# Routed experts' rows added into the second layer's rows by the gathering transfers, and the loads of two lanes released by the last expert's product, in a two-layer decoder kernel

## The chip, the cores and the metric

The kernel runs on one core of one Trainium2 chip. The metric is the device time of one execution in microseconds; several executions are timed, and one more is run under the profiler. The engines are TensorE (PE), VectorE (DVE), ScalarE (ACT), GpSimd (POOL) and SyncE (SP, which only issues transfers here). Each takes its instructions in the order in which they are written; semaphores hold them until what they need is there. A transfer that GpSimd issues can fetch its rows by a table of row numbers (a gather).

## What is computed

Two decoder layers on x of 8 x 256 rows of 256 values. Layer 1 ends with a feed-forward part of routed experts; layer 2 takes its sum, normalised, through attention by Fourier transforms, cross attention and a feed-forward part with three-valued weights.

```python
def _L0_ffn_ref(...):
    x = hidden_states.reshape(-1, Dm)
    logits = x @ router_w
    expert_idx = jnp.argmax(logits, axis=-1)
    score = jax.nn.sigmoid(jnp.max(logits, axis=-1))
    xs = x * score[:, None]
    for e in range(n_experts):
        m = (expert_idx == e)[:, None]
        xe = jnp.where(m, xs, 0.0)
        h = jax.nn.silu(xe @ gate_w[e]) * (xe @ up_w[e])
        out = out + jnp.where(m, h @ down_w[e], 0.0)
    shared = jax.nn.silu(x @ shared_gate_w) * (x @ shared_up_w) @ shared_down_w
    return (out + shared)

x = _layernorm(x + _L0_attn_ref(x, ...), axis=-1)
x = _layernorm(x + _L0_xattn_ref(x, ctx_512, ...), axis=-1)
x = _layernorm(x + _L0_ffn_ref(x, ...), axis=-1)
x = _layernorm(x + _L1_attn_ref(x, ...), axis=-1)
x = _layernorm(x + _L1_xattn_ref(x, ctx_512, ...), axis=-1)
x = _layernorm(x + _L1_ffn_ref(x, ...), axis=-1)
```

The change touches the third of these lines: the sum of x, the shared part and the routed part, and its layer norm.

## The kernel before

**Units and lanes.** The rows are cut into 8 units of 256 rows (one batch entry each), held as 128 partitions x 2 rows of 256 values. Layer 1 works on units 0 to 7. Layer 2 works on the same rows as units 8 to 15. A lane is the set of on-chip tiles that one unit uses; layer 2 has four lanes, for units 8 to 11; units 12 to 15 reuse them. The lanes of units 8 and 9 lie in the area that the profile calls `wide`, those of 10 and 11 in `first`.

**Experts.** Layer 1 leaves, per unit, x plus the shared part in the DRAM tensor `x_mid` (the mid stores), and sends each row to a slot of `sent_rows` by its expert. 23 tiles of 128 such rows then go through `x_t` (transpose), `x_gu`, `x_h`, `x_b` (transpose), `x_dn` (product back), `x_out` (ScalarE's copy) and `x_st` (SyncE's store to the DRAM tensor `made_rows`). Tile 22 is the last. `made_at` says for each row of a unit where in `made_rows` its result lies.

**Into layer 2.** For unit u, in before:

- `ld` (SyncE) loads the unit's rows of `x_mid` into B.y, once all made rows and all mid stores have landed (`opened`), and for units 12 to 15 once the lane's former unit has had its last normalised rows made (`ln_x` of u-4, part 3);
- `gt` (GpSimd, L2314 on) gathers the unit's rows of `made_rows` by two indirect transfers into a tile of its own, B.got, once the same stores have landed, and for units 12 to 15 once the lane's former `res` part 0 has read B.got;
- `res` part 0 (VectorE, L1969) adds: B.y = B.y + B.got, once both have landed;
- `ln` (VectorE, L1927 to L1933) takes the statistics, `ln_pow` (GpSimd, L2275 and L2277) the power -1/2, `ln_x` (ScalarE, L1647) the normalised rows;
- `turn` part 0 (TensorE, L1077 with c_identity) transposes them, `ft` (L1070 with w_dft_hi) takes the Fourier transform, `nr` and `nk` normalise it (GpSimd's L2371 and L2376), `cs` (L1476) sums along the rows, `cs_v` (GpSimd L2383 to L2385), `vt` and `proj` part 1 go back; then come `q` (L1070 with w_lq_hi), `sc`, `ex`, `pv` and `proj` part 2 of cross attention, and `gu` (L1494), `hf` and `proj` part 3 (L1252) of the feed-forward part.

**Weights made meanwhile.** The weights of layer 2 are made on the chip from the inputs, in eight parts by heads and columns. `ha` (L1144), `hk`, `hw`, `hb`, `hc` fold the cross attention's matrices for a pair of heads (heads 6 and 7 are the last). `f_16`, `f_sc` and `f_gt` (VectorE L1910 to L1919), `f_q` (GpSimd L2332 to L2339, four instructions for a part), `fw` and `fw_c` make the three-valued weights. `ld_f` and `ld_h` are their loads; a wide area of the chip's memory is shared, so that `ld_f` or `ld_h` waits for an earlier `fw_c`.

**The order.** Every step above is one part in `lay_plan()`, with an engine, a length and the parts that it follows. `p.settle(n_banks, passes, seed)` lays the parts out and so draws the order of the instructions on every engine at once; the seed shakes their urgency. The emitters then write each engine's instructions in that order. `keep_warm` puts dummy matmuls (`bank<-c_all_ones`, L1461) where the layout shows TensorE idle. A change of one number in the table can thus move instructions everywhere.

## Time and profile before

| | before |
|---|---|
| median of three runs | 640.63 us (639.15 to 644.22) |
| the profiled execution, own time | 638.61 us |
| its span in the profile | 637.3 us |
| mean granted clock of TensorE | 0.979 |
| TensorE matmul busy | 574.4 us (90%) |
| VectorE busy | 480.8 us (75%) |
| ScalarE busy | 386.7 us (61%) |
| GpSimd busy | 374.3 us (59%) |

The span is the stretch that the profile shows; the execution's own time has 1.3 us around it. Busy shares are means over stages that are bound by different things: layer 1 to 210 us, mostly the experts' tiles from 210 to 284, the first tokens of layer 2 from 284 to 335, and from there layer 2 with all lanes filled. The timelines name an instruction by its start, its length, its line, the tile that it writes and those that it reads; a bracket gives how long its engine sat idle before it and what ended that.

### The profile page before, as it was taken

The numbers are of one execution on the slowest core, as the hardware profiler recorded it, in microseconds if no ns is written. First come the engines' busy times: TensorE is split into PE (matmuls) and PEld (weight loads), VectorE is DVE, ScalarE is ACT, GpSimd is POOL, SyncE is SP. The second block draws the span as 40 slices with busy tenths as digits, with TensorE's granted clock in tenths as the row PEclk, the third lists the DMA queues.
The fourth block names the chain that finished last, engine by engine and source line by source line (L and its number), as shares of the span: only waits on it lengthen the run. The fifth ranks groups of instructions, "written<-read, shape, count | busy, mean of one in ns | idle before, by whom it ended". The sixth has DMA issues, their size and how long they took to land. (4 is left out here: it accounts for less than half of the span.)

```text
span 637.3 us, 14620 instructions
## 1 busy us (share of the span) xinstructions
PE 574.4 (90%) x5400; PEld 445.5 (70%) x5400; DVE 480.8 (75%) x1286; ACT 386.7 (61%) x826; POOL 374.3 (59%) x468
## 2 busy tenths in 40 slices
PE   5789989988889799876989999999999999999995
PEld 4656767767666465553546888886788768889894
DVE  4673767776688798866779877697988997876656
ACT  3668667667766455541765565665747655655763
POOL 3436445556783267578998654572675634333896
PEclk9999999999899899998989999999999999999999
DMA  9753221102455244426211000001000000000001
GB/s 257 231 147 80 60 84 60 42 19 68 141 145 163 76 124 150 126 92 182 79 38 35 1 2 2 7 29 35 1 9 27 14 21 2 1 2 2 2 1 67
DMA packets 50418, 41.75 MB, mean 66 GB/s; under 512 B 15642, under 2 KB 48924, under 8 KB 50332
## 3 DMA queue, kind: packets, MB, share of 16 engines
q1 hardware_dynamic: 46444, 35.08, 18.6%
q0 software_dynamic: 1536, 4.20, 2.1%
q10 hardware_dynamic: 2368, 1.54, 0.9%
q8 instruction: 44, 0.72, 0.5%
q14 instruction: 26, 0.21, 0.1%
HBM read 31.49 MB, written 10.35 MB: 66 GB/s over the span
## 5 line engine op out<-in xcount | busy, mean ns | idle before, releaser
L1821 DVE TENSOR_TENSOR first<-bank,first 128x512 f16<-128x512 f32 (+3 forms) x141 | 76.1, 556 | 22.5 <-ACT first L1656 5.9
L2297 POOL TENSOR_TENSOR first<-first 128x512 f16<-128x512 f32 x44 | 51.9, 1181 | 42.4 <-ACT first L1708 32.6
L1077 PE MATMUL bank<-c_identity,first 128*128 128x128 f32 (+1 forms) x353 | 58.9, 284 | 9.2 <-DMA first<-in_x 3.1
L1070 PE MATMUL bank<-wide,first 128*128 (+4 forms) x199 | 54.2, 282 | 11.9 <-DVE first L1821 5.1
L1077 PEld LDWEIGHTS bank<-c_identity,first 128*128 128x128 f32 (+1 forms) x353 | 40.3, 141 | 20.3 <-DMA first<-in_x 3.7
L1071 PE MATMUL bank<-wide,first 128*128 (+4 forms) x199 | 53.8, 280 | 0.0
L1072 PE MATMUL bank<-wide,first 128*128 (+4 forms) x199 | 52.9, 279 | 0.0
L2275 POOL TENSOR_TENSOR first<-first,minus_half 128x2 f32<-128x2 f32 x30 | 21.6, 719 | 46.5 <-DVE first L1933 46.5
L1077 PE MATMUL bank<-c_identity,wide 128*128 128x128 f32 (+3 forms) x203 | 34.1, 291 | 9.2 <-DMA c_all_ones<-const_all_ones 7.1
L1821 DVE TENSOR_TENSOR wide<-bank,wide 128x512 f16<-128x512 f32 (+3 forms) x57 | 35.0, 635 | 9.0 <-ACT wide L1687 3.5
L1070 PEld LDWEIGHTS bank<-wide,first 128*128 128x128 f16 (+1 forms) x199 | 19.2, 98 | 24.6 <-issue 16.5
L1647 ACT ACTIVATE wide<-wide 128x256 f32<-128x256 f32 x32 | 17.4, 593 | 31.0 <-POOL wide L2277 30.9
L1077 PEld LDWEIGHTS bank<-c_identity,wide 128*128 128x128 f32 (+3 forms) x203 | 23.9, 146 | 16.2 <-DMA c_all_ones<-const_all_ones 7.1
L1700 ACT ACTIVATE first<-bank 128x512 f16<-128x512 f32 x44 | 26.2, 596 | 11.1 <-PE bank L1328 5.4
L1998 DVE TENSOR_REDUCE first<-bank 128x8 f32<-128x512 f32 x44 | 27.6, 681 | 6.1 <-PE bank L1290 3.7
L2332 POOL TENSOR_TENSOR wide<-wide 128x768 bf16<-128x768 bf16 x8 | 13.1, 1642 | 31.5 <-DVE wide L1919 31.5
L1494 PE MATMUL bank<-first,w_fgu 128*128 128x256 f16 x256 | 29.8, 273 | 0.6 <-DVE first L2219 0.6
L1494 PE MATMUL bank<-wide,w_fgu 128*128 128x256 f16 x256 | 30.1, 273 | 0.0
L2396 POOL TENSOR_TENSOR wide<-wide 128x512 f16<-128x512 f32 x16 | 18.6, 1161 | 19.0 <-ACT wide L1797 19.0
L1708 ACT ACTIVATE first<-bank 128x512 f32<-128x512 f32 x44 | 26.3, 597 | 5.7 <-POOL first L2297 5.5
L2297 POOL TENSOR_TENSOR wide<-wide 128x512 f16<-128x512 f32 x16 | 18.5, 1158 | 17.9 <-ACT wide L1708 15.4
L1070 PE MATMUL bank<-first,wide 128*128 128x256 f16 (+1 forms) x98 | 25.9, 271 | 2.4 <-DVE first L1821 2.4
(471 smaller groups left out, 2106.3 us busy)
## 6 DMA issues: line engine op xcount, KB each, us to landing
first<-sent_rows SPq DMA_DIRECT2D x20, 128.0 KB, 2.0
made_rows<-first SPq DMA_DIRECT2D x20, 128.0 KB, 1.8
wide<-in_L_ffn_gate_w SPq DMA_DIRECT2D x8, 256.0 KB
wide<-in_L_ffn_up_w SPq DMA_DIRECT2D x8, 256.0 KB
wide<-in_L_ffn_down_w SPq DMA_DIRECT2D x8, 256.0 KB
wide<-in_L_xattn_Wq SPq DMA_DIRECT2D x8, 256.0 KB
wide<-in_L_xattn_Wo SPq DMA_DIRECT2D x16, 128.0 KB
wide<-in_L_ffn_w_gate_up SPq DMA_DIRECT2D x8, 256.0 KB
```

Source lines behind the costliest of these rows:

```text
L1070: mm(o, lhs[0], rhs[0], start=start, stop=False)
L1071: mm(o, lhs[0], rhs[1], start=False, stop=False)
L1072: return mm(o, lhs[1], rhs[0], start=False, stop=stop)
L1077: last = nc.tensor.transpose(view[0:m, c0:c0 + n], src, kc["identity" if dt == F32 else "identity_bf"][0:n, 0:n])
L1494: last = mm(b[:, n * S:(n + 1) * S], k.w_fgu[:, c, at:at + P], B.xT[part][:, c, :], start=(c == 0 and part == 0), stop=(c == C - 1 and par ...
L1700: fn(lane(u).ph[g % 2], scores(u, g)[:, :], ACT.Exp, scale=0.25 if u < NB else 1.0).then_inc(says("ex_h"), 1)
L1708: fn(lane(u).pf, scores(u, g)[:, :], ACT.Exp, scale=0.25 if u < NB else 1.0).then_inc(says("ex_f"), 1)
L1821: return V.tensor_tensor(lo, whole, hi, ALU.subtract)
L1998: V.tensor_reduce(o, b, AX.X, ALU.max).then_inc(says("max_v"), 1)
L2275: pool.step(G.tensor_tensor(B.rstd, B.rstd, k.minus_half, ALU.pow))
L2297: G.tensor_tensor(B.pl[r], B.pf, B.ph[r], ALU.subtract).then_inc(says("ex_l"), 1)
L2396: G.tensor_tensor(lo, B.hf, hi, ALU.subtract).then_inc(says("hf_lo"), 1)
```

## The change

B.got is gone. The gather of a unit waits for the unit's own load and then adds the rows of `made_rows` into B.y on the way (`compute_op=ALU.add`). The eight adds of `res` part 0 are gone, and `ln` part 0 waits for the gather. The loads of units 8 and 9 no longer wait for the made rows, but for the last expert's product `x_dn` 22 and the mid stores; those of 10 to 15 wait as before. A few lengths in the planner's table are changed (`f_sc` 170 to 185, `f_gt` 195 to 186, `rt_xs` 140 to 114, `tb_tok` 498 to 560, left out of the diff below), and the order is drawn with 38 passes and seed 81.

```diff
--- before.py
+++ after.py
@@ -499,9 +499,10 @@
             return (name, o, g) if o is not None else None
 
         gate = [("x_in_st", n, 0) for n in range(NT)] + [("in_mid", v, 0) for v in every]
-        p.add("gt", u, 0, "POOL", 200, gate + [("tb_tok", 0, 0), old("res", 0)], k)
-        p.add("in_gt", u, 0, "AIR", 200, [("gt", u, 0)])
-        p.add("ld", u, 0, "SP", 45, gate + [("in_mid", i, 0), old("ln_x", 3)], k)
+        p.add("gt", u, 0, "POOL", 200, gate + [("tb_tok", 0, 0), ("in", u, 0)], k)
+        p.add("in_gt", u, 0, "AIR", 220, [("gt", u, 0)])
+        over = [("x_dn", NT - 1, 0)] + [("in_mid", v, 0) for v in every] if i < 2 else gate
+        p.add("ld", u, 0, "SP", 45, over + [old("ln_x", 3)], k)
         p.add("in", u, 0, "AIR", 250, [("ld", u, 0)])
         p.add("ld_ctx", u, 0, "SP", 90, gate + [old("rope")], k)
         p.add("in_ctx", u, 0, "AIR", 250, [("ld_ctx", u, 0)])
@@ -510,8 +511,7 @@
         p.add("kd_lo", u, 0, "POOL", 43, [("kd_hi", u, 0)], k)
         chain("kt", u, 0, [("rope", u, 0), old("sc", 3)], k, pe=20, hi=29, lo=28)
 
-        p.add("res", u, 0, "DVE", 70, [("in_gt", u, 0), ("in", u, 0)], k)
-        norm(u, 0, k)
+        norm(u, 0, k, "in_gt")
         chain("turn", u, 0, [("ln_x", u, 0)], k)
         for t in range(T):
             p.add("ft", u, t, "PE", 136, [("turn_lo", u, 0), ("pd_lo", 0, 0), ("pd_lo", 0, 1)], k, 1, ("ft_raw", u, t) if t else ("nr", u, 0))
@@ -568,7 +568,7 @@
         p.add("res", u, 3, "DVE", 122, [("rm_pow", u, 0), ("proj", u, 3)], k)
         norm(u, 3, k)
         p.add("st", u, 0, "SP", 45, [("ln_x", u, 3)], k)
-    p.settle(8, 37, 38)
+    p.settle(8, 38, 81)
     p.keep_warm(80, 0.7, 900)
     return p
 
@@ -808,7 +808,7 @@
             return v if dt == F32 else v.bitcast(dt)
 
         tn = "p (t n) -> p t n"
-        B.x, B.y, B.got = (tile([T, D]) for m in range(3))
+        B.x, B.y = (tile([T, D]) for m in range(2))
         B.xT = (tile([C, S], F16), tile([C, S], F16))
         B.ctx, B.kv, B.rot = (tile([DC]) for m in range(3))
         B.kv2 = tile([P])
@@ -988,7 +988,12 @@
                 sp.wait_ge(*done("rt_xs", u - FIRST))
             load(B.x, unit_rows(A["x"], u), dma["x"][u % FIRST])
         else:
-            opened(u)
+            if u < NB + 2:
+                sp.wait_ge(*done("x_dn", NT - 1))
+                for n in range(FIRST):
+                    sp.wait_ge(dma["mid"][n], 16 * turns_of(n))
+            else:
+                opened(u)
             if u >= NB + LANES:
                 sp.wait_ge(*done("ln_x", u - LANES, 3))
             load(B.y, unit_rows(k.x_mid, u - NB), dma["x"][u % LANES])
@@ -1920,7 +1925,10 @@
 
     def ln(u, n):
         B = lane(u)
-        dve.wait_ge(*done("proj" if u < NB and n < 2 else "res", u, n))
+        if u >= NB and n == 0:
+            dve.wait_ge(dma["got"][u % LANES], 32 * visit(u))
+        else:
+            dve.wait_ge(*done("proj" if u < NB and n < 2 else "res", u, n))
         dve.wait_ge(*done("pm_pow", 0))
         y = summed_rows(k, u, n)
         for t in range(T):
@@ -1963,10 +1971,6 @@
         if u < NB:
             dve.wait_ge(*done("proj", u, n))
             last = V.scalar_tensor_tensor(B.y, bank("proj", u, n)[:, :].rearrange(tn, t=T), 0.5, B.x, ALU.mult, ALU.add)
-        elif n == 0:
-            dve.wait_ge(dma["x"][u % LANES], 16 * (turns_of(u % LANES) + visit(u)))
-            dve.wait_ge(dma["got"][u % LANES], 32 * visit(u))
-            last = V.tensor_tensor(B.y, B.y, B.got, ALU.add)
         elif n < 3:
             dve.wait_ge(*done("proj", u, n))
             last = V.scalar_tensor_tensor(B.y, bank("proj", u, n)[:, :].rearrange(tn, t=T), 1.0, B.x, ALU.mult, ALU.add)
@@ -2315,11 +2319,10 @@
         B, i = lane(u), u - NB
         opened()
         pool.wait_ge(*done("tb_tok", 0))
-        if u >= NB + LANES:
-            pool.wait_ge(*done("res", u - LANES, 0))
+        pool.wait_ge(dma["x"][u % LANES], 16 * (turns_of(u % LANES) + visit(u)))
         for s in range(T):
-            G.indirect_dma_start(B.got[:, s, :], None, k.made[:, :], bass.IndirectOffsetOnAxis(ap=k.made_at[:, i * T + s:i * T + s + 1], axis=0)
-                                 ).then_inc(dma["got"][u % LANES], 16)
+            G.indirect_dma_start(B.y[:, s, :], None, k.made[:, :], bass.IndirectOffsetOnAxis(ap=k.made_at[:, i * T + s:i * T + s + 1], axis=0),
+                                 compute_op=ALU.add).then_inc(dma["got"][u % LANES], 16)
 
     def f_q(u, n):
         i, step = n // 4, n % 4
```

All engines' orders differ. Line numbers of the changed kernel are 5 higher for VectorE, ScalarE and TensorE and 3 to 5 higher for GpSimd. The rows below are those of the three places of which the prediction speaks. In them `d_x0` to `d_x3` are the semaphores of the lanes' loads, `d_made` and `d_mid` those of the stores, `s_ln` that of the statistics, and a row is one instruction or a run of equal ones.

GpSimd between the last tiles of the experts and the first tokens of layer 2, before (L2332 to L2339 are `f_q`, L2321 the gathers of units 8, 9 and 10, L2275 `ln_pow`):

```order
L2339 TENSOR_TENSOR wide<-wide 128x768 [waits s_f_q]
L2321 DMA wide<-made_rows,made_at 128x256 [waits d_mid0,d_made6,d_mid1,d_made5,d_mid2,d_made4,d_mid3,d_made3,d_mid4,d_made2,s_table_dve,d_made1,d_made0]
L2321 DMA wide<-made_rows,made_at 128x256 x3
L2321 DMA first<-made_rows,made_at 128x256 x2
L2332 TENSOR_TENSOR wide<-wide 128x768 [waits s_ternary_dve]
L2275 TENSOR_TENSOR wide<-wide,minus_half 128x2 [waits s_ln]
L2277 TENSOR_TENSOR wide<-wide 128x2 [waits s_ln,own_pool]
L2335 TENSOR_TENSOR wide<-wide 128x768 [waits s_f_q]
L2337 TENSOR_TENSOR wide<-wide 128x768 [waits s_f_q]
L2275 TENSOR_TENSOR wide<-wide,minus_half 128x2 [waits s_ln]
```

The same place in the changed kernel (L2335 to L2342 are `f_q`, L2324 the gathers, L2279 `ln_pow`, L2350 on `rope` of unit 8):

```order
L2340 TENSOR_TENSOR wide<-wide 128x768 [waits s_f_q]
L2324 DMA wide<-made_rows,made_at 128x256 [waits d_mid0,d_mid1,d_made6,d_mid2,d_made5,d_mid3,d_made4,d_mid4,d_made3,s_table_dve,d_made2,d_x0,d_made1,d_made0]
L2324 DMA wide<-made_rows,made_at 128x256
L2342 TENSOR_TENSOR wide<-wide 128x768 [waits s_f_q]
L2324 DMA wide<-made_rows,made_at 128x256 [waits d_x1]
L2324 DMA wide<-made_rows,made_at 128x256
L2324 DMA first<-made_rows,made_at 128x256 [waits d_x2]
L2324 DMA first<-made_rows,made_at 128x256
L2279 TENSOR_TENSOR wide<-wide,minus_half 128x2 [waits s_ln]
L2281 TENSOR_TENSOR wide<-wide 128x2 [waits s_ln,own_pool]
L2350 MEMSET wide 128x256 [waits d_ctx0]
L2351 CAST wide<-c_half_rows 128x2
```

The gathers wait one by one for the lanes' loads, one `f_q` instruction stands among them instead of behind them, and `ln_pow` of unit 8 follows the third gather at once, with `rope` of unit 8 behind it.

SyncE at the same place, before (from the last stores of made rows to the loads of head 6's matrices; the `wide<-in_L_ffn` rows are the loads of feed-forward part 7):

```order
L897 DMA made_rows<-first 128x256 [waits s_expert_act] x2
L897 DMA wide<-in_L_ffn_w_gate_up 128x2x256 [waits s_fw_c]
L897 DMA wide<-in_L_ffn_w_proj 128x128 x2
L897 DMA made_rows<-first 128x256 [waits s_expert_act] x2
L897 DMA wide<-x_mid 128x2x256 [waits d_made5,d_made4,d_made6,d_made3,d_mid1,d_made2,d_mid2,d_made1,d_made0]
L897 DMA wide<-x_mid 128x2x256
L897 DMA first<-x_mid 128x2x256
L897 DMA wide<-in_ctx 64x64 x2
L897 DMA wide<-in_L_xattn_w_kc_q 128x2x192 [waits s_fw_c]
```

And in the changed kernel:

```order
L897 DMA made_rows<-first 128x256 [waits s_expert_act] x5
L897 DMA wide<-x_mid 128x2x256 [waits d_mid2,d_mid1,s_expert_pe]
L897 DMA made_rows<-first 128x256 [waits s_expert_act]
L897 DMA wide<-x_mid 128x2x256
L897 DMA wide<-in_L_ffn_w_gate_up 128x2x256 [waits s_fw_c]
L897 DMA wide<-in_L_ffn_w_proj 128x128 x2
L897 DMA first<-x_mid 128x2x256 [waits d_made4,d_made3,d_made5,d_made2,d_made6,d_made1,d_made0]
L897 DMA wide<-in_ctx 64x64 x2
L897 DMA first<-x_mid 128x2x256
L897 DMA wide<-in_ctx 64x64 x2
```

The load of unit 8 stands ahead of the last store of made rows and waits for TensorE's count of expert products; a load of feed-forward weights is behind the stores instead of ahead of them; the loads of head 6 are further down.

TensorE from the last expert's product on, before (the dummies are L1461, L1144 is `ha` of head 6; L1077 with c_identity are transposes, among them those of unit 8, L1070 with w_dft_hi begins `ft` of unit 8):

```order
L1461 MATMUL bank<-c_all_ones 128x512 [waits s_expert_act]
L1461 MATMUL bank<-c_all_ones 128x512 x11
L1077 MATMUL bank<-c_identity_bf,wide 128x128 [waits s_f_q]
L1077 MATMUL bank<-c_identity_bf,wide 128x128 x5
L1461 MATMUL bank<-c_all_ones 128x512 [waits s_expert_act]
L1461 MATMUL bank<-c_all_ones 128x512 x26
L1144 MATMUL bank<-wide 96x256 [waits d_stage0]
L1144 MATMUL bank<-wide 96x256 x3
L1077 MATMUL bank<-c_identity,wide 128x128 [waits s_ln_x]
L1077 MATMUL bank<-c_identity,wide 128x128 x3
L1077 MATMUL bank<-c_identity,wide 128x64 [waits s_fw_c]
L1077 MATMUL bank<-c_identity,wide 128x128 x4
```

And in the changed kernel:

```order
L1082 MATMUL bank<-c_identity_bf,wide 128x128 [waits s_expert_act,s_f_q]
L1082 MATMUL bank<-c_identity_bf,wide 128x128 x5
L1466 MATMUL bank<-c_all_ones 128x512 x22
L1082 MATMUL bank<-c_identity_bf,wide 128x128 [waits s_f_q]
L1082 MATMUL bank<-c_identity_bf,wide 128x128 x5
L1466 MATMUL bank<-c_all_ones 128x512 [waits s_expert_act]
L1466 MATMUL bank<-c_all_ones 128x512 x17
L1082 MATMUL bank<-c_identity,wide 128x128 [waits s_ln_x]
L1082 MATMUL bank<-c_identity,wide 128x128 x3
L1082 MATMUL bank<-c_identity,wide 128x128 [waits s_expert_act,s_rope]
L1466 MATMUL bank<-c_all_ones 128x512 x8
L1075 MATMUL bank<-w_dft_hi,wide 128x512 [waits s_turn_lo]
```

The fold of head 6 no longer stands between the dummies and the transposes of unit 8; two transposes of feed-forward parts stand there among the dummies.

GpSimd at the reload of unit 12's lane in the changed kernel (L2279 and L2281 ahead of the gather are `ln_pow` of unit 8's last part, L2399 `hf_lo` of unit 9, L2301 `ex_l` of unit 10):

```order
L2416 TENSOR_TENSOR wide<-wide,minus_half 128x2 [waits s_rm_v]
L2279 TENSOR_TENSOR wide<-wide,minus_half 128x2 [waits s_ln]
L2281 TENSOR_TENSOR wide<-wide 128x2 [waits s_ln,own_pool]
L2324 DMA wide<-made_rows,made_at 128x256 [waits d_x0]
L2324 DMA wide<-made_rows,made_at 128x256
L2399 TENSOR_TENSOR wide<-wide 128x512 [waits s_hf_hi]
L2301 TENSOR_TENSOR first<-first 128x512 [waits s_ex_f,s_ex_h]
L2399 TENSOR_TENSOR wide<-wide 128x512 [waits s_hf_hi]
L2279 TENSOR_TENSOR wide<-wide,minus_half 128x2 [waits s_ln]
```

In before all the gathers of units 12 to 15 stand much earlier, right behind the `rope` steps of units 8 to 11. Now each stands where its lane's load can be expected, with its wait for that load, and other units' steps are behind it on GpSimd.

## Rows read from the trace of the kernel before

**Rows 1.** windows: length, busy of PE, PEld, DVE, ACT, POOL, then clock

```profile
210.00:284.00 74.00, 64.62 (x414) 40.29 (x415) 61.71 (x131) 39.36 (x109) 42.30 (x27) 0.98 0.37 112
284.00:335.00 51.00, 41.65 (x220) 22.78 (x219) 34.75 (x97) 26.18 (x60) 45.12 (x75) 0.90 0.36 103
335.00:604.00 269.00, 263.49 (x2452) 219.62 (x2450) 218.13 (x570) 165.35 (x315) 148.88 (x190) 1.00 0.04 11
```

**Rows 2.** TensorE's waits, 210:284 and 284:335: total us, times, longest

```profile
PE bank L1070 <- DVE first L1821: 3.7, 3, 2.5
PE bank L1144 <- DMA wide<-in_L_xattn_W_qr: 5.3, 1, 5.3
```

**Rows 3.** timeline of TensorE, 283 to 336: start and length, us

```profile
283.62 0.27 PE L1072 MATMUL bank<-wide,first 128*128 x1
...
298.26 3.73 PE L1144 MATMUL bank<-wide 128*96 128x256 f32 x8 [5.34 <-DMA wide<-in_L_xattn_W_qr]
301.78 1.98 PE L1077 MATMUL bank<-c_identity,wide 128*128 128x128 f32 x9
...
304.71 0.39 PE L1070 MATMUL bank<-w_dft_hi,wide 128*128 128x512 f16 x1
...
315.72 0.38 PE L1476 MATMUL bank<-wide,c_up_to 128*128 128x256 f16 x2
...
335.43 0.27 PE L1070 MATMUL bank<-wide,w_lq_hi 128*128 128x256 f16 x1
```

**Rows 4.** timeline of POOL, 284 to 315

```profile
284.89 1.64 POOL L2339 TENSOR_TENSOR wide<-wide 128x768 bf16<-128x768 bf16 x1
288.00 1.02 POOL L2321 DMA_INDIRECT wide<-made_rows,made_at  x1 [1.47 <-DMA made_rows<-first]
289.32 1.11 POOL L2321 DMA_INDIRECT wide<-made_rows,made_at  x1 [0.30 <-issue]
...
297.04 1.19 POOL L2275 TENSOR_TENSOR wide<-wide,minus_half 128x2 f32<-128x2 f32 x1
...
305.36 0.31 POOL L2347 MEMSET wide<- 128x256 bf16 x1
...
307.00 0.88 POOL L2357 TENSOR_SCALAR wide<-wide,c_half_rows 128x64 f32<-128x64 f32 x2
...
314.19 1.15 POOL L2376 TENSOR_TENSOR wide<-wide 128x512 f16<-128x512 f32 x1
```

**Rows 5.** timelines of VectorE and of ScalarE, 293 to 299

```profile
293.31 0.69 DVE L1969 TENSOR_TENSOR wide<-wide 128x512 f32<-128x512 f32 x1 [2.86 <-DMA wide<-made_rows,made_at]
298.54 1.09 ACT L1647 ACTIVATE wide<-wide 128x256 f32<-128x256 f32 x2 [10.54 <-POOL wide L2277]
```

**Rows 6.** lines L1969, L2321 by themselves: ns min/median/max, first and last start

```profile
L1969 DVE TENSOR_TENSOR first<-first x4: 683/1326/1635, 299.0 to 511.0; 128x512 f32<-128x512 f32 x4
L2321 POOL DMA_INDIRECT first<-made_rows,made_at x8: 945/950/1081, 293.2 to 346.6; - x8
...
DMA to landing us min/median/max: 2.7/3.2/4.5
```

**Rows 7.** the page's DMA issues: KB each, median us to landing

```profile
first<-sent_rows SPq DMA_DIRECT2D x20, 128.0 KB, 2.0
first<-x_mid SPq DMA_DIRECT2D x4, 256.0 KB, 3.7
```

**Rows 8.** timeline of VectorE, 273 to 280, first and last of five

```profile
273.87 0.94 DVE L1910 TENSOR_REDUCE wide<-wide 128x12 f32<-128x768 bf16 x1
...
278.87 0.95 DVE L1919 SCALAR_TENSOR_TENSOR wide<-wide 128x768 bf16<-128x768 bf16 x1
```

**Rows 9.** timelines of TensorE, SyncE, ScalarE at unit 14's reload

```profile
468.03 3.65 PE L1252 MATMUL bank<-w_fp,first 128*128 128x256 bf16 x32
476.14 0.36 SPq L897 DMA_DIRECT2D first<-x_mid  x1
483.30 1.10 ACT L1647 ACTIVATE first<-first 128x256 f32<-128x256 f32 x2
```

More of the change, by code:

```diff
@@ L388, in lay_plan @@
             p.add("f_16", 0, i, "ACT", 82, [("in_f", 0, i)], rank)
-            p.add("f_sc", 0, i, "DVE", 170, [("f_16", 0, i)], rank)
-            p.add("f_gt", 0, i, "DVE", 195, [("f_sc", 0, i)], rank)
+            p.add("f_sc", 0, i, "DVE", 185, [("f_16", 0, i)], rank)
+            p.add("f_gt", 0, i, "DVE", 186, [("f_sc", 0, i)], rank)
             for n2 in range(4):
```

4 lines of the change are left out of this document (2 added, 2 removed).

## The prediction

> **What bounds the kernel now.** I read four views, in this order: the table of windows (where each engine is busy), the waits of TensorE by window, the timeline of each engine around 284 us, and the timeline around one reload of a lane.
>
> The windows split the span by stage. From 335 to 604 us TensorE is busy 263.49 of 269 us at the full clock: the second layer's attention and feed-forward parts are bound by its work. Nothing that another engine gets rid of there can save more than the 5.5 us that it idles. From 210 to 284 us (the experts' tiles) it idles 9.4 us, and from 284 to 335 us (I call it the bridge: first tokens of layer 2) 9.4 us, though its 41.65 busy us hold dummy matmuls too [rows 1]. So time can be won in the expert stage and in the bridge. The waits say what ends last: in the expert stage VectorE's split L1821, 3.7 us; in the bridge the wait for W_qr, 5.3 us [rows 2].
>
> The bridge on TensorE runs so: the last expert product x_dn(22) issues its last matmul at 283.62 and ends at X = 283.89. The next real work of length (head 6's fold, L1144) starts at 298.26, the transposes of unit 8 (turn 8) at 301.78, its Fourier product (ft 8) at 304.71, its running sum (cs 8) at 315.72, and the first query product (q 8), from which TensorE no longer idles, at 335.43 = X+51.5 [rows 3]. POOL issues the six gathers of units 8 to 10 from 288.00, then one quantising op (1.64 us each), and ln_pow 8 only at 297.04 [rows 4]. The row of the first says that the last made rows released it, 1.47 us after POOL was free. VectorE starts the add for unit 8 at 293.31, 2.86 us idle for the gather; ACT's ln_x 8 starts at 298.54, 1.3 us after ln_pow [rows 5]. So the chain is: product, store, gather, add, statistics, POOL's queue, ln_x, transposes, with the fold of head 6 (3.73 us) pushed ahead of the transposes.
>
> **The change part by part.**
>
> *The add.* Eight L1969 adds go, 0.68 to 1.64 us each [rows 6], some 9 us of VectorE in all. VectorE has room in 335 to 604 (218.13 busy of 269 [rows 1]), so that is worth nothing by itself; only the add on the chain of unit 8 (0.69) counts, and one in each reload of a lane. I keep it there.
>
> *Earlier loads.* Loads of units 8 and 9 now wait only for x_dn(22), not for the made rows. They are free by X and land by about X+3.7 (a 256 KB load takes 3.7 [rows 7]), before the last made rows are there: in before POOL's first gather, released by them, starts at 288.00 = X+4.1 [rows 4]. So unit 8's gather waits for nothing new; but in before the add had load and gather side by side, and a load was never last there. This part is worth nothing in itself: it pays for the gather's new wait. The load stands ahead of the last store on SP; in exchange a weight load (part 7's) that stood ahead of that store has gone behind it. I take the first gather at X+3.8, 0.3 better.
>
> *The order of the bridge.* All engines' orders were drawn anew. On POOL, gathers 8, 9, 10 have one quantising op among them and ln_pow 8 directly behind, so one quantising op less ahead of it. First gather X+3.8; its pair needs 2.5 us (288.00 to 290.73 is two and a gap), lands as in before 4.0 after the second start (289.32 to 293.31 [rows 4, 5]), so at X+9.1; VectorE's statistics take 1.3 more, X+10.4. POOL is not free then: three pairs 7.5 us and one op of 1.6 give X+12.9, at most X+14; ln_pow ends by X+14.2 (1.3), ln_x takes 1.1, and turn 8 starts at X+15.2 with nothing ahead of it on TensorE (before X+17.9). ft 8 at X+17.2 against X+20.8: 3.6 us won. But then POOL has rope 8 (2.5, from 305.36 to 307.88), four quantising ops (6.5), ln_pow 9 (0.9), four more (6.5) and nk_lo 8 itself (1.15) to do [rows 4]: from X+14.2 that is X+31.8, and cs 8, which needs nk_lo 8, comes no earlier than before (315.72 - 283.89 = 31.8). The folds of heads 6 and 7 stand after cs 8 now, and the 5.3 us for W_qr fall into time in which their loads have long landed. From there on I lay the changed order of TensorE and POOL out with before's durations and find q 8 at X+49.5: 2.0 us won. Bounds: nothing won (POOL sets it), 3.6 won (ft 8's gain is kept).
>
> *Behind q 8.* The part of ft 10 that before does at 318.89 to 324 is done after q 8 in the changed order, and the parts behind q 8 add up to 2.1 us more: +2.1, sure, as this stage is bound by TensorE [rows 1].
>
> *The expert stage.* The quantising of feed-forward part 3 (f_sc, f_gt) stood on VectorE between the last tiles: five instructions from 273.87 to 279.82: 0.94, 1.60, 0.17, 0.95 and 0.95, 4.6 us in all [rows 8], in front of splits for which TensorE waits [rows 2]. It is behind x_dn(22) now. TensorE waited for VectorE 3.7 us by L1821 in this window, so I take half of 4.6: -2.3, bounds 0 and -4.6.
>
> *Reloads of a lane.* Units 12 to 15 take the tiles of 8 to 11. Before, the gathers stood ready long before in their own tile (issued by 346 us [rows 6]); now they must wait for the load, and the load for ln_x(u-4,3). In before, for unit 14: product ends at 471.68 (468.03 + 3.65), load is issued at 476.14, ln_x runs at 483.30, so rows are ready at 484.4, 12.7 us after the product [rows 9]; there turn 14 came just then. Now: 4.5 + 3.7 (load) + 1.3 (second gather's start) + 2.7 to 4.5 (landing [rows 6]) + 1.3 + 0.9 + 1.1 = 15.5 to 17.3 us. The changed order leaves other work of TensorE between product and transposes: counted in parts with 0.11 us per matmul of 256 columns (32 in 3.65 [rows 9]), 20.0, 17.0, 20.8 and 15.7 us for units 12 to 15. So units 12 and 14 are covered, units 13 and 15 just or not: +1.5 in all, bounds 0 and +6 (the 1.6 at unit 15, with an engine's queue of 1 to 2 us at each of the four). Behind the gather of unit 12 POOL holds ex_l of unit 10; it comes 12.5 us after the product, TensorE has 15.5 us of work before it needs it, so this is covered by 3 us.
>
> *What an adding transfer costs.* No row shows one. From below: as the plain gather, 2.7 to 4.5 us from issue to landing [rows 6]. From above: it reads its destination too, 128 KB more; 128 KB more cost 1.7 us between the loads of 128 KB (2.0) and 256 KB (3.7) [rows 7]. I take the lower end, since 2.0 for 128 KB and 3.7 for 256 KB are loads of other forms and a gather has never waited for its data here; the upper end is rival 4, which puts 1.7 us on three gathers and the sum at 643.0 instead of 637.9. The Trainium skill (Collectives: The Full Stack, Part 3) speaks for the upper end: an add in a transfer costs nothing in itself but needs two source reads, and a reduce ran at 32.35 GB/s where a copy ran at 62.28. No run here shows it yet.
>
> Dummy matmuls are 3 fewer and fill idle time only: 0.
>
> **The sum.** 638.61 (the profiled execution) - 2.3 (experts) - 2.0 (bridge) + 2.1 (work behind) + 1.5 (reloads) = 637.9. The median of the runs is 640.63, 2.0 above that execution, so 639.9; I forecast **640 us**.
>
> **Rivals.**
> 1. *Faster by more than that.* The whole 4.6 us of quantising were on the path and the 3.6 us of ft 8 are kept, reloads cost nothing: 638.61 - 4.6 - 3.6 + 2.1 = 632.5, and up to 1 more from waits that went, so 633 to 634 on the median. For it: 9.4 us of idling in each of the two stages [rows 1]. Against it: POOL is busy nearly all the time in the bridge (45.12 of 51 us [rows 1]), and has no less to do.
> 2. *Slower: the reload chain.* Load and gather in series stall TensorE at the reloads. It decides where the chain is longer than the other work: over 15.7 us for unit 15, 17.0 for 13, 20 for 12 and 14. If each engine's queue adds 2 us and the adding transfer 1.7, the chain is 19.5 to 21: stalls of 4.5, 3.3, 0.5 and 0.3, near 9 us in all: 638.61 - 0 + 2.1 + 9 - 2 = 647.7, 649 on the median with no gain among the experts. For it: in before the chain of 12.7 us had 13.5 between product and transposes, so little slack is usual. Against it: the series' mean case fits.
> 3. *The bridge gains nothing,* since POOL sets cs 8 and what is behind it: 638.61 - 2.3 + 2.1 + 1.5 = 639.9, 642 on the median.
> 4. *The adding transfer reads twice,* 1.7 us each by the rows above: at unit 8 it is on the chain, at two reloads too: 637.9 + 1.7 + 3.4 = 643.0, 645 on the median. The Trainium skill's rule above would have it so.
>
> **Chances.** Forecast 0.37, rival 1 0.25, rival 2 0.20, rival 3 0.10, rival 4 0.08. About 1% (6.4 us) is what a measurement of this kernel can tell from no change. Only rival 1 is faster by more than that (below 634.2; just), only rival 2 slower (above 647.0): faster 0.25, same 0.55, slower 0.20. The range reaches to both, as neither can be left out with 0.45 of the chance: 631 to 649; the forecast's own range is 636 to 645 (bounds of its terms: -4.6, -3.6, +6 cannot all meet). New orders in the first 210 us are in that range too: I found no term there.
>
> **What would show it.** Right, if in the changed profile turn 8 starts about X+15, cs 8 about X+32 and the first L1075 with w_lq_hi about X+49.5; if SP's load of unit 8 starts at X and POOL's gather about X+3.8; if the wait for W_qr is gone from TensorE's waits; if the gathers of units 12 to 15 start 4 us after their loads, and TensorE's waits from q 8 to 604 stay near 7 us. Wrong, if the gathers land later than 4.5 us after issue, if TensorE waits for ln_x at the reloads with more than 2 us each, or if the expert stage is as long as it was (X at 283.9).

## The result and the profile after

| | before | changed |
|---|---|---|
| median of 12 runs each | 642.39 us | 646.61 us |
| ratio, 95% interval | | 1.0076 (1.005 to 1.0102) |
| the profiled executions, span | 637.3 us | 642.1 us |
| last expert product ends (X) | 283.89 | 279.57 |
| first query product (q 8) | 335.43 = X + 51.5 | 335.19 = X + 55.6 |
| last matmul ends | 630.26 | 635.52 |

The changed kernel is 0.76% slower, and the interval leaves no room for a gain. The forecast was 0.1% faster; 646.61 lies in the range and inside the 1% that was called "same", but the sign was wrong. Twelve executions of each kernel told 0.76% from nothing, so the prediction's "about 1%" was too coarse. Single executions of the changed kernel spread by 1 to 2%, and one of its later profiles (653.7 us) fell on a slow one. Forecast and profile agree in one thing only: in both the time lies in three places, X, the stretch from X to q 8, and what is behind it.

The changed kernel's table of windows (stretch, length, busy us of TensorE, its loads, VectorE, ScalarE, GpSimd, then the granted clock, DMA share, GB/s), to hold against [rows 1]:

```profile
210.00:284.00 74.00, 65.04 (x422) 41.44 (x423) 55.02 (x123) 37.21 (x104) 36.67 (x23) 1.00 0.37 111
284.00:335.00 51.00, 38.73 (x207) 21.25 (x204) 32.74 (x91) 23.34 (x50) 47.63 (x63) 0.90 0.39 87
335.00:604.00 269.00, 260.30 (x2414) 216.06 (x2413) 211.43 (x569) 164.78 (x320) 157.22 (x201) 1.00 0.06 13
```

VectorE has 6.7 us less work before 284 (4.6 was forecast; X lies 4.3 us earlier here, so the windows don't hold quite the same steps), and GpSimd is busy 47.6 of 51 us in the bridge, 2.5 more than before, with fewer instructions (63 for 75). Behind 335 TensorE idles 8.7 us instead of 5.5. What GpSimd does with its time stands on the gathers' line, which answers to [rows 6]:

```profile
L2324 POOL DMA_INDIRECT wide<-made_rows,made_at x8: 1532/1556/1662, 284.2 to 454.9; - x8
L2324 POOL DMA_INDIRECT first<-made_rows,made_at x8: 1550/1575/1678, 293.2 to 510.6; - x8
...
DMA to landing us min/median/max: 3.7/3.9/3.9
```

An adding gather holds GpSimd 1.55 us; a plain one held it 0.95. It lands 3.9 us after its issue instead of 3.2. The page's line for the software queue differs too:

```profile
q0 software_dynamic: 3072, 4.20, 3.3%
```

In before that line reads 1536 packets for the same 4.20 MB and 2.1%. These count layer 1's 16 scatters too, so the 1536 more in the changed kernel all belong to the 16 gathers: 96 more packets each, for no more bytes. That the longer issue is spent on them is an inference. The timeline of GpSimd around the bridge, to hold against [rows 4]:

```profile
284.20 1.63 POOL L2324 DMA_INDIRECT wide<-made_rows,made_at  x1 [1.03 <-DMA made_rows<-first]
286.14 1.55 POOL L2324 DMA_INDIRECT wide<-made_rows,made_at  x1 [0.31 <-issue]
287.14 2.22 POOL L2342 TENSOR_TENSOR wide<-wide 128x768 bf16<-128x768 bf16 x1
289.52 1.53 POOL L2324 DMA_INDIRECT wide<-made_rows,made_at  x1 [0.16 <-issue]
...
296.08 1.32 POOL L2279 TENSOR_TENSOR wide<-wide,minus_half 128x2 f32<-128x2 f32 x1
```

A pair takes 3.7 us (289.52 to 293.21) where 2.5 was reckoned, and ln_pow 8 follows the sixth gather at X + 16.5. VectorE's row of the last statistics instruction of unit 8 stands at 292.37, 3.7 us before: the statistics had long been ready, GpSimd was not. On TensorE the same stretch reads, against [rows 3]:

```profile
279.74 4.91 PE L1466 MATMUL bank<-c_all_ones 128*128 128x512 f16 x22
289.42 0.82 PE L1082 MATMUL bank<-c_identity_bf,wide 128*128 128x128 bf16 x6 [4.77 <-POOL wide L2342]
290.04 5.39 PE L1466 MATMUL bank<-c_all_ones 128*128 128x512 f16 x18
298.85 0.65 PE L1082 MATMUL bank<-c_identity,wide 128*128 128x128 f32 x4 [3.42 <-ACT wide L1652]
300.18 0.47 PE L1082 MATMUL bank<-c_identity,wide 128*128 128x128 f32 x1 [0.67 <-POOL wide L2360]
300.44 3.15 PE L1466 MATMUL bank<-c_all_ones 128*128 128x512 f16 x8
303.43 0.38 PE L1075 MATMUL bank<-w_dft_hi,wide 128*128 128x512 f16 x1
```

The wait for W_qr is gone, as forecast. In its place stand 4.77 and 3.42 us behind dummies, both of GpSimd's making, and eight dummies of 0.39 us each: 22 of them took 4.91 us at 279.74 (0.22 each, the clock at 2.4 GHz), these took 3.15 with a granted clock of 0.57 over them, most of it the lower level. Turn 8 came at X + 19.3 (forecast X + 15.2, before X + 17.9), ft 8 at X + 23.9 (forecast 17.2, before 20.8), q 8 at X + 55.6 (forecast 49.5, before 51.5).

### The profile page after: what moved, and what is told of

The parts are those of the page before. It is cut to its first block, busy times and chain, and to the rows that moved or that the text cites. A ratio compares the mean times of both kernels' runs of the same rounds, so it can differ in the third digit from the quotient of the medians.

```text
span 642.1 us, 14592 instructions
## 1 busy us (share of the span) xinstructions
PE 573.2 (89%) x5397; PEld 444.2 (69%) x5397; DVE 465.8 (73%) x1278; ACT 385.1 (60%) x826; POOL 383.4 (60%) x468
## 3 DMA queue, kind: packets, MB, share of 16 engines
q0 software_dynamic: 3072, 4.20, 3.3%
## 4 chain that ended last, share of the span: by engine, by line
PE 43%; POOL 9%; DVE 7%; ACT 6%; DMA 4%; issue 3%; another core or an unknown queue 1%; SPq 1%; POOLq 0%; DVEq 0%
PE bank L1075 8%; PE bank L1077 7%; PE bank L1076 7%; PE bank L1499 6%; PE bank L1257 4%; PE bank L1082 4%; POOL wide L2324 2%; DMA wide<-in_L_ffn_down_w 1%; POOL first L2324 1%; DVE first L1826 1%; DMA wide<-x_mid 1%; PE bank L1358 1%; DVE stats L1935 1%; PE bank L1360 1%
## 5 line engine op out<-in xcount | busy, mean ns | idle before, releaser
L2301 POOL TENSOR_TENSOR first<-first 128x512 f16<-128x512 f32 x44 | 51.3, 1171 | 38.4 <-ACT first L1713 34.4
L1082 PE MATMUL bank<-c_identity,first 128*128 128x128 f32 (+2 forms) x353 | 57.9, 280 | 6.2 <-ACT first L1652 3.4
L1077 PE MATMUL bank<-wide,first 128*128 (+4 forms) x199 | 52.7, 278 | 0.0
L1082 PEld LDWEIGHTS bank<-c_identity,first 128*128 128x128 f32 (+2 forms) x353 | 39.7, 139 | 14.7 <-ACT first L1652 4.9
L1082 PE MATMUL bank<-c_identity,wide 128*128 128x128 f32 (+3 forms) x203 | 33.8, 287 | 13.1 <-DMA c_all_ones<-const_all_ones 7.2
L2279 POOL TENSOR_TENSOR first<-first,minus_half 128x2 f32<-128x2 f32 x30 | 22.4, 745 | 33.7 <-DVE first L1941 33.6
L2335 POOL TENSOR_TENSOR wide<-wide 128x768 bf16<-128x768 bf16 x8 | 13.1, 1638 | 36.8 <-DVE wide L1924 36.8
L2399 POOL TENSOR_TENSOR wide<-wide 128x512 f16<-128x512 f32 x16 | 19.1, 1195 | 18.2 <-ACT wide L1802 18.2
L1499 PEld LDWEIGHTS bank<-first,w_fgu 128*128 128x128 bf16 x256 | 24.8, 98 | 4.4 <-DVE first L1826 1.0
L1499 PEld LDWEIGHTS bank<-wide,w_fgu 128*128 128x128 bf16 x256 | 24.9, 98 | 3.0
```

Of the source, the lines that this page charges most:

```text
L1077: return mm(o, lhs[1], rhs[0], start=False, stop=stop)
L1082: last = nc.tensor.transpose(view[0:m, c0:c0 + n], src, kc["identity" if dt == F32 else "identity_bf"][0:n, 0:n])
L1499: last = mm(b[:, n * S:(n + 1) * S], k.w_fgu[:, c, at:at + P], B.xT[part][:, c, :], start=(c == 0 and part == 0), stop=(c == C - 1 and par ...
L2279: pool.step(G.tensor_tensor(B.rstd, B.rstd, k.minus_half, ALU.pow))
L2301: G.tensor_tensor(B.pl[r], B.pf, B.ph[r], ALU.subtract).then_inc(says("ex_l"), 1)
```

## The experiments

Theory A: the adding gathers are what costs, by holding GpSimd. Theory B: the new order costs. Theory C: load and gather in series at the reloads cost (rival 2). All ratios are to the kernel before, timed beside each on the same chip, with 95% intervals. The runs e1 to e4 were on one chip; r1, r2, e5 and e6 on a second; e7 to e9 on a third; e10 and r3 to r5 on a fourth. Only ratios of one chip are compared closely, for a reason that stands under the repeats.

**Plain gathers in the changed order.** Every engine's order and every wait is the changed kernel's; the gather is plain again, into B.got, and VectorE adds.

```diff
-            G.indirect_dma_start(B.y[:, s, :], None, k.made[:, :], ..., compute_op=ALU.add)
+            G.indirect_dma_start(B.got[:, s, :], None, k.made[:, :], ...)
 in ln(), part 0 of units 8 to 15:
             dve.wait_ge(dma["got"][u % LANES], 32 * visit(u))
+            dve.step(V.tensor_tensor(B.y, B.y, B.got, ALU.add))
```

> The changed kernel's order on every engine and all its waits, but the gathers are plain, into a tile of their own (B.got), and VectorE adds before it takes the statistics (8 adds back). Theory A (the adding gather holds GpSimd longer: 1.55 us against 0.95 us an issue, 16 of them, six in a row between the experts and layer 2): an issue is back at 0.95, ln_pow of unit 8 comes about 4 us earlier after the last expert product (X+13 instead of X+16.7), q 8 at about X+51 to X+52 instead of X+55.8, and the span is 4 to 6 us shorter than the changed kernel's 642.1: 636 to 638. Theory B (the new order is what costs): span within 1.5 us of 642.1. Theory C (load and gather in series cost, whoever adds): also within 1.5 us, since the series is kept.

Measured: 0.9953 (0.9922 to 0.9983), 1.2% under the changed kernel's ratio of the first occasion, span 634.6. ln_pow 8 came at X + 15.5 and q 8 at X + 53.3, 1 to 2.5 us later than expected. Later, repeated beside the changed kernel on one chip:

> The run e1_plain_gather again: 0.990 to 0.998 of before; the last expert product ends where it does in the run above within 2 us, as the code up to there is the same; 53 to 54 us from there to q 8, 299 to 301 behind it.

> The changed kernel a third time, for a profile on the same chip as the two below. From the last expert product to q 8 55 to 57 us, behind q 8 300 to 303 us.

Measured: plain 0.9936 (0.9894 to 0.9978), changed 1.0011 (0.9973 to 1.0048), 0.75% apart. q 8 came at X + 51.9, 1 to 2 us earlier than expected. Theory A holds: on one chip the adding transfers cost 0.75%, about 5 us, and without them the new order is 0.5 to 0.6% faster than the kernel before, on two chips. So neither theory B nor theory C is the cause of the loss in this order. GpSimd in the plain run (r4):

```profile
279.05 1.02 POOL L2325 DMA_INDIRECT wide<-made_rows,made_at  x1 [0.76 <-DMA made_rows<-first]
280.37 0.96 POOL L2325 DMA_INDIRECT wide<-made_rows,made_at  x1 [0.30 <-issue]
281.35 1.64 POOL L2342 TENSOR_TENSOR wide<-wide 128x768 bf16<-128x768 bf16 x1
283.15 0.96 POOL L2325 DMA_INDIRECT wide<-made_rows,made_at  x1 [0.16 <-issue]
...
288.73 0.84 POOL L2280 TENSOR_TENSOR wide<-wide,minus_half 128x2 f32<-128x2 f32 x1
```

From the first gather to ln_pow 8 it is 9.7 us here and 12.6 in the changed kernel beside it (279.77 to 292.35). The stretch from the first gather to q 8 shows the price most cleanly, since what lies ahead of the first gather can't be the gathers' doing. Here it is for the runs of this section and those below, with GpSimd's busy time in it:

| first gather to q 8 | us | GpSimd busy | clock |
|---|---|---|---|
| before (r5) | 47.8 | 43.5 | 0.96 |
| before's order, adding (e5) | 51.0 | 46.7 | 0.87 |
| changed (r3) | 51.7 | 48.6 | 0.87 |
| plain gathers (r4) | 47.6 | 44.3 | 0.93 |
| plain, GpSimd held (e7) | 48.9 | 46.4 | 0.90 |
| changed, more dummies (e10) | 51.6 | 47.9 | 0.97 |

In one order GpSimd idles the same with and without adding (3.2 us in r3 and r4, 4.3 in e5 and r5): what its work grows by, the stretch grows by. That is 4.2 us in the changed order (3.4 by the first profile, with 51.0 us and 47.8 of work) and 3.3 in the order of before.

**No wait for the load.** The same, and the gather waits for ln_pow(u-4, 0) instead of the unit's load; VectorE waits for both.

```diff
-        pool.wait_ge(dma["x"][u % LANES], 16 * (turns_of(u % LANES) + visit(u)))
+        if u >= NB + LANES:
+            pool.wait_ge(*done("ln_pow", u - LANES, 0))
```

> As the run above, but the gather no longer waits for the unit's load (for units 12 to 15 it waits for ln_pow of the unit before it in the lane instead); VectorE's add waits for both. The order on every engine stays that of the changed kernel. Theory C (series at the reloads of a lane costs): TensorE's waits behind q 8, 9.2 us in the changed kernel against 5.5 in before, fall by 2 to 4 us against the run above and so does the span. Theory A: the series is worth under 1 us, this run and the one above agree within 1 us.

Measured: 0.9927 (0.9897 to 0.9958), 0.26% under the run before it, intervals overlapping. TensorE's waits from q 8 to 600 fell from 8.1 to 7.0 us. Theory C is worth about 1 us of waits in this order; the profile doesn't show it as time, as the stretch from q 8 to the last matmul was 302.0 us there and 299.6 in e1.

**Plain for units 8 to 11 only.** 

```diff
+            into = B.got if u < NB + LANES else B.y
+            G.indirect_dma_start(into[:, s, :], ..., **(dict() if u < NB + LANES else dict(compute_op=ALU.add)))
```

> The changed kernel's order and waits, plain gathers and VectorE's add for units 8 to 11 only; units 12 to 15 keep adding gathers. Theory A: nearly all of the gain of the plain gathers is in the stretch between the experts and q 8, as there eight gathers stand in front of other work of GpSimd: 3 to 5 us shorter than the changed kernel. If the reloads are what costs, under 1.5 us.

Measured: 0.9981 (0.9952 to 1.001). On the same chip none adding was 0.9953, so the last eight cost 0.3%, not resolved. All sixteen cost 0.75% on the fourth chip, which leaves about 0.5% for the first eight (an estimate, from two chips).

**Gathers of units 9 and 10 moved behind other work of GpSimd.**

```diff
     p.settle(8, 38, 81)
+    (in p.order["POOL"]: gt 9 moved behind rope 8, gt 10 behind ln_pow 9)
```

> The changed kernel with adding gathers; on GpSimd alone the gather of unit 9 is moved behind rope of unit 8 and the gather of unit 10 behind ln_pow of unit 9. Theory A: ln_pow 8 comes 7 us earlier (two pairs of 3.7 us are out of its way, though it waits for the statistics until X+13), turn 8 about 3 to 4 us earlier, but GpSimd has the same sum of work before cs 8, so q 8 comes 0 to 2 us earlier and the span is 0 to 2 us shorter. If ln_pow 8 is what holds q 8: 3 to 4 us shorter.

Measured: 1.0194 (1.0152 to 1.0236), 1.2% above the changed kernel's 1.0076 and 1.8% above its 1.0011 of r3: 8 to 12 us slower where 0 to 2 faster was expected. ln_pow 8 did come early (X + 13), turn 8 at X + 15.9, close to the times that the prediction had for the changed kernel. But the order on VectorE was left, and there ln 9 and ln 10 stand ahead of turn_lo 8 and now wait for the moved gathers (8.5 and 7.0 us). TensorE's row:

```profile
308.78 0.61 PE L1082 MATMUL bank<-w_dft_hi,wide 128*128 128x512 f16 x1 [15.37 <-DVE wide L1833]
```

An order drawn for all engines at once can't be mended on one of them.

**Adding gathers in the order of before.** Units 8 to 11 add and wait for their load, a small write stands for each dropped add; units 12 to 15 as before.

```diff
+        else:
+            pool.wait_ge(dma["x"][u % LANES], 16 * (turns_of(u % LANES) + visit(u)))
+            adds = dict(compute_op=ALU.add) if u < NB + LANES else dict()
```

> The kernel before, its order on every engine, but the gathers of units 8 to 11 add into B.y and wait for the unit's load (their four adds on VectorE are gone, each a small write in its place); units 12 to 15 as before. Theory A: eight issues of 1.55 us for 0.95 on GpSimd, six of them ahead of ln_pow 8: ln_pow 8 at X+16 to X+17 instead of X+13.2, q 8 later by 2 to 4 us, ratio to before 1.003 to 1.008. If the adding transfer costs nothing where the order was made without it: within 0.2%.

Measured: 1.0078 (1.004 to 1.0116). The old order with eight adding gathers is as slow as the changed kernel. X to q 8 is 57.2 us (51.5, 50.7 and 51.2 in three profiles of before), and behind q 8 nothing moved (294.3 against 294.3 to 294.8). But two things changed in this run: the gathers add, and they wait for loads that are still issued as late as in before. Its first gather:

```profile
297.48 1.64 POOL L2325 DMA_INDIRECT wide<-made_rows,made_at  x1 [3.56 <-DMA wide<-x_mid]
```

It starts at X + 6.2, released by the load; in before it starts at X + 3.3 to X + 4.1, released by the made rows. So of some 6 us, 2 to 3 are the wait for the load, which the changed kernel avoids by its earlier loads, and 3.3 are the adding (the table above). That is also why ln_pow 8 came at X + 18.2 where X + 16 to 17 was expected. The window 300 to 320 of this kernel:

```profile
300.00:320.00 20.00, 11.84 (x47) 6.24 (x46) 5.22 (x23) 6.30 (x14) 18.29 (x23) 0.66 0.44 82
```

GpSimd is busy; behind it TensorE is busy 11.8 us, with a granted clock of 0.66. Over the same steps of before's third profile (X + 8.7 to X + 28.7, as X lay 7 us later here) it is busy 14.1 us at 0.91.

**Other draws.** The kernel before and the changed kernel with seed 1, and the latter with plain gathers.

```diff
-    p.settle(8, 37, 38)
+    p.settle(8, 38, 1)
```

> The kernel before with another draw of the order (38 passes, seed 1), nothing else. If a draw alone moves the time as much as the change did, the ratio lies outside 0.995 to 1.005; I expect slower, 1.000 to 1.015, as seed 38 was left standing in the code among others.

> The changed kernel drawn with seed 1 (38 passes). Against the kernel before with the same seed (0.987 of before): if the adding gathers cost what they cost with the changed kernel's own seed (1.2%), about 0.995 to 1.005 of before; but the two plans differ, and another draw alone moved the time by 1.3%, so 0.99 to 1.02 is all that can be said.

> The run above with plain gathers and VectorE's add, its order kept: 0.5 to 1.3% faster than the run above, as in the changed kernel's own order (e1 against the changed kernel). If the cost of the adding gathers hangs on the one order, under 0.3%.

Measured: before with seed 1 0.9873 (0.9825 to 0.992), which beats every other kernel here; changed with seed 1 1.0102 (1.0066 to 1.0138); the same with plain gathers 0.9937 (0.9906 to 0.9969). Before with seed 1 had been expected to be slower and was faster. So a draw alone moves the time by 1.3%, more than the whole change. With seed 1 on both sides the change costs 2.3% (over two chips), and on one chip the adding gathers cost 1.65%. From the first gather to q 8 they cost 3.3 us here (50.6 and 47.3), but behind q 8 another 6.5 (306.3 and 299.8 us). There the reloads matter: TensorE's wait for the normalised rows behind q 8, adding, then plain:

```profile
PE bank L1082 <- ACT first L1652: 3.9, 1, 3.9
```

```profile
PE bank L1082 <- ACT first L1652: 1.6, 1, 1.6
```

Behind the wait of 3.9 us the granted clock was 0.55 from 524.4 to 530 us and then 1.00 again; behind that of 1.6 it stayed at 1.00. So the same 2684 matmuls were busy 294.2 us in the one and 290.3 in the other: the wait costs its own length and the slow clock behind it.

**GpSimd held without adding.** Plain gathers in the changed order, with two small writes behind each of the first eight.

```diff
+            if u < NB + LANES:
+                G.memset(B.fill[:, s, :], 0.0)
+                G.memset(B.fill[:, 2 + s, :], 0.0)
```

> The run e1_plain_gather (the changed kernel's order, plain gathers, VectorE's add) with two small writes of zeros to a tile of their own (128x128 each) behind every gather of units 8 to 11 on GpSimd, 16 in all. They hold GpSimd about 0.4 to 0.5 us a gather, of the 0.6 to 0.7 by which an adding gather holds it longer, and nothing else changes; the plain transfer lands as early as before. If GpSimd's hold is what the adding gathers cost: ln_pow 8 about 2.5 us later after the last expert product than in e1 (15.5 there), q 8 1.5 to 3 us later, 0.2 to 0.5% above e1. If the later landing (3.9 against 2.8 us) is the cost: as e1.

Measured: 1.0029 (0.9995 to 1.0062), 0.8% above the two plain runs of other chips. From the first gather to ln_pow 8 it is 10.5 us (9.7 without), and from the first gather to q 8 48.9 (47.6): 1.3 us for 2.1 of GpSimd's work (46.4 for 44.3). A hold without any adding costs time, so the later landing isn't needed to explain the loss. The rest of the 0.8% is not the hold's: X was 281.4 in its profile, though the code up to there is the same.

**More dummies.** The changed kernel with five runs of dummies in the bridge made 1.6 times as long.

```diff
-    max(1, int(share * idle / 22))
+    max(1, int(share * idle / 22 * (1.6 if p_from < at < p_to else 1)))
```

> The changed kernel with its five runs of dummy matmuls between the last expert product and cs 8 made 1.6 times as long (35, 29, 13, 8 and 18 for 22, 18, 8, 5 and 11), nothing else. There TensorE waited 4.8 and 3.4 us behind dummies and the granted clock was 0.84 from 300 to 320 us. If half of what the adding gathers cost is the slower clock that follows longer idling: granted clock above 0.95 from 300 to 320, and 1 to 4 us faster than the changed kernel (ratio to before 1.001 to 1.006). If the clock is no cause: the same as the changed kernel (1.007), or slower by dummies that stand in the way.

Measured: 1.0058 (1.0018 to 1.0097), against 1.0011 for the changed kernel on the same chip: no gain. The ratio lies in the band that was named for the other outcome, but only because the kernel to beat was at 1.0011 there and not at 1.007. Its window 300 to 320, then that of the changed kernel (third profile):

```profile
300.00:320.00 20.00, 18.87 (x116) 10.81 (x115) 14.38 (x37) 12.53 (x28) 18.60 (x17) 1.00 0.35 93
```

```profile
300.00:320.00 20.00, 17.58 (x95) 9.59 (x94) 13.56 (x38) 11.11 (x24) 19.37 (x18) 0.91 0.35 93
```

The clock stayed up (1.00 for 0.91, and 0.97 for 0.87 from the first gather to q 8), and that stretch was no shorter (51.6 and 51.7 us); the kernel was not faster. Before's other two profiles say the same: 47.4 us there with clocks of 0.89 and 0.93, where r5 has 47.8 with 0.96. In the bridge the slower clock goes along with the loss and is no part of it that these runs show; GpSimd's work is.

**Repeats for the parts of the sum.**

> The changed kernel again, on the same chip as the three below. Theory A, as the plain gathers left it: 4 to 8 us slower than the run e1_plain_gather was against before, so 0.5 to 1.0% above before; the last expert product ends at 273 to 276 as in four other runs of the same code up to there, and not at 279.6 (that run showed a granted clock of 0.84 from 180 to 200 us). If 279.6 belongs to this kernel, it comes again.

> The kernel before again, for a second profile. Its last expert product ended at 283.89; if the new order wins the expert stage by itself, it ends at 280 or later again; if 283.9 was an accident of that execution, at 275 to 278.

> The kernel before a third time, for a profile on the same chip: the last expert product ends 4 to 9 us later than in the two runs above if the new order is faster up to there, within 2 us if it is not.

Measured: the changed kernel again 1.0069 (1.0027 to 1.0111) on the second chip, and 1.0011 (r3, above) on the fourth; before again 0.9997 and 1.0013. So the changed kernel is 0.7% slower on two occasions and the same on a third. X of before's code is 283.9, 284.8 and 284.3, and 291.3 in e5 (granted clock 0.95 up to 284 us for 0.97 to 0.98). The code of the changed order up to X gave 273.0 to 275.3 in seven profiles (0.99 to 1.00), 279.6 and 281.4 in two (0.98 and 0.97), and 283.8 in r1, where 273 to 276 was expected. Seven and three are two different courses. The window 180 to 200 and TensorE's wait for L1614 (a copy of ScalarE's) in the changed kernel's first profile, then in e1:

```profile
180.00:200.00 20.00, 14.72 (x108) 9.90 (x107) 11.25 (x51) 8.98 (x23) 9.25 (x8) 0.84 0.51 151
PE bank L1163 <- ACT wide L1614: 4.7, 2, 4.2
```

```profile
180.00:200.00 20.00, 17.84 (x148) 12.53 (x144) 18.24 (x68) 12.60 (x33) 10.70 (x10) 1.00 0.56 164
PE bank L1163 <- ACT wide L1614: 1.3, 2, 0.9
```

In the three long profiles TensorE waited 4.2 to 4.7 us there, about 190 us, and the granted clock was 0.76 to 0.81 from 195 to 210; in the seven it waited at most 1.0 us at a time and the clock stayed at 1.00. From the first load of the experts' rows to X it is 79.1 to 80.0 us in the seven and 85.1 to 85.7 in the three (82.1 to 83.2 in before, 84.8 in e5). What makes ScalarE late is not shown. The changed kernel has this wait in the profiles of the two occasions on which it is 0.7% slower, and not in that of the third: the wait may be what the occasions differ by, but it was not switched on and off by any run. Of the expectations of r3 to r5, q 8 missed by 0.3 us in r3 and by 1.1 in r4, and X of before came 9.6 to 10.1 us later where 4 to 9 was named. On one chip:

| us | before (r5) | changed (r3) | plain gathers (r4) |
|---|---|---|---|
| X | 284.3 | 274.2 | 274.7 |
| X to q 8 | 51.2 | 57.3 | 51.9 |
| q 8 to the end of the last matmul | 294.3 | 300.2 | 299.8 |
| behind it | 7.1 | 6.7 | 6.7 |
| span | 636.9 | 638.3 | 633.0 |

## Why the prediction was wrong, point by point

**The adding transfer's cost** is the step that failed. The prediction said "from below: as the plain gather", took that end, and put the upper end (rival 4) on the landing only: "1.7 us on three gathers". What it never priced was the issue on GpSimd, for which it used the plain gather's 1.25 us from start to start. Measured, an adding issue is 1.55 us for 0.95, a pair 3.7 for 2.5, and the landing comes 3.9 for 3.2 us after issue: the landing's 0.7 was smaller than rival 4's 1.7, the issue's 0.6 was not in the sum at all, and it counts six times ahead of ln_pow 8 and eight times ahead of q 8. From the first gather to q 8 that cost 4.2 us (51.7 against 47.6). The prediction itself had GpSimd as the engine that held ln_pow 8, "45.12 of 51 us" busy, and still asked only when the data land. The Trainium skill (Collectives: The Full Stack, Part 3) says of a collective's reduce that its add needs two source reads. The trace agrees in part: the adding gathers take more packets (3072 for 1536 in the software queue), but the queue's bytes stay at 4.20 MB, so the second read itself is not seen, and no run here measured a rate. The price was in the issue on GpSimd, of which that section does not speak.

**The bridge**, forecast at -2.0 with bounds 0 and -3.6, was +4.1 in the first pair of profiles and +6.1 on one chip. With plain gathers in the same order it is +0.7. Of the 5.4 us between, 4.2 are the adding gathers and 1.2 lie ahead of the first gather, which started at X + 5.6 and X + 4.4, released by the made rows both times (X + 4.4 to X + 5.8 in all ten profiles of this order, adding or not; X + 3.8 was forecast). The reckoning without adding missed by 2.7: 0.9 of it is the later first gather, and from there to q 8 the new order is as long as the old one (47.6 and 47.8 us). So rival 3 had this part right: GpSimd's work sets it. The "one quantising op less" ahead of ln_pow 8 was a misreading too; both orders have one between the first gather and ln_pow 8. A bound on the side of a loss was missing: the bounds ended at "nothing won", and no reason was given.

**The expert stage**, forecast at -2.3, was -4.3 in the first pair and -10.1 on one chip. Its mechanism (quantising moved off VectorE) may fit a part: from the first load of expert rows to X it was 83.2 us before and 79.1 in the changed kernel on that chip, -4.1, within its bounds. The other 6.0 us lie ahead of the first load (201.1 against 195.1 us), in layer 1, where the prediction said "I found no term there". In the first pair the gain was all in layer 1 (200.8 to 193.9 us, -6.9) and the experts' stretch was 2.6 us longer (83.1 to 85.7), with the wait at 190 us and the slow clock behind it. So the -4.3 there, which looks like the forecast's gain, is luck: its mechanism doesn't show in it. No run put the quantising back alone.

**Behind q 8**, forecast at +2.1 of work and +1.5 of stalls at the reloads, was +5.5 in the first pair and +5.8 on one chip, and +5.5 with plain gathers. TensorE's waits from q 8 to 600 us are 4.9 before, 8.2 in the changed kernel, 8.1 plain, 7.0 plain without the wait for the load. So 3.3 us are stalls (1.5 were forecast), and two thirds of them come with the order, not with the series of load and gather. The series itself is about as long as forecast. Unit 14's reload in the changed kernel, to hold against [rows 9] (the timelines of SyncE, GpSimd and ScalarE):

```profile
487.98 0.36 SPq L897 DMA_DIRECT2D first<-x_mid  x1
```

```profile
491.87 1.64 POOL L2324 DMA_INDIRECT first<-made_rows,made_at  x1 [0.17 <-issue]
493.81 1.55 POOL L2324 DMA_INDIRECT first<-made_rows,made_at  x1 [0.31 <-issue]
```

```profile
500.00 1.09 ACT L1652 ACTIVATE first<-first 128x256 f32<-128x256 f32 x2 [2.33 <-POOL first L2281]
```

From load to rows 13.1 us where before took 8.3 and the forecast's terms give 11.0 to 12.8, and TensorE waits for such rows 0.5 us in all behind q 8: the other work covers it in this order. In the order of seed 1 it does not (3.9 us at one reload, with the slow clock behind it), which is rival 2's mechanism: 6.5 us behind q 8 where it had 9.

**The earlier loads** of units 8 and 9 were said to be worth nothing and to pay for the gather's new wait. No run takes them alone out of the changed kernel, but e5 has adding gathers without them, and its first gather waited for the load to X + 6.2. **The adds** on VectorE were called worth nothing but for the chain; with them back the kernel is 0.75% faster, so they cost less than what replaced them.

**The sum**: -10.1 (of which 6.0 unseen, 4.1 for 2.3) + 6.1 (for -2.0) + 5.8 (for +3.6) - 0.4 = +1.4 on one chip. In that sum errors of about 8 us of both signs nearly cancelled, which is why the result lies in the range and yet proves little: that is luck. Rival 2 named the right sign by the wrong place for this order; rival 4 named the right cause, the adding transfer, with the wrong price in the wrong step.

## What to carry to other kernels

Moving an add from VectorE into a gathering transfer moves its price to the engine that issues the transfer. Read that engine's share in the stretch before anything else: where GpSimd is the queue that all wait in, 5.6 us off a VectorE with room are no gain for 7.3 us more on GpSimd (busy times of r3 against r4). When an edit redraws the whole schedule, time the edit in the old schedule and the schedule without the edit; here the first cost 0.8% (its new wait included) and the second won 0.5 to 0.6%, and another seed alone won 1.3%. Measure a stretch from the event that the edit can first touch (here the first gather): from X on, the parts that the edit can't touch varied by over 1 us.
